# Rotary projection as 128 stationary columns: weight halves side by side, summed by VectorE

## The reference, cut to what matters

```python
x = layernorm(x)                      # (8, 512, 512)
c_kv = x @ W_DKV + b_DKV              # 512 -> 128
c_q  = x @ W_DQ  + b_DQ               # 512 -> 128
k_c, v_c, q_c = c_kv @ W_UK + b_UK, c_kv @ W_UV + b_UV, c_q @ W_UQ + b_UQ
k_r = (x @ W_KR + b_KR) * pe          # 512 -> 32, the rotary part, shared by 16 heads
q_r = (x @ W_QR + b_QR) * pe          # 512 -> 32
k = concat([k_c per head, k_r]);  q = concat([q_c per head, q_r])
attn = softmax(q @ k.T / sqrt(32));  ctx = attn @ v_c;  y = ctx @ W_O + b_O
```

## Time and profile before

| | us |
|---|---|
| median of 3 runs | 1569.3 (1569.14 to 1573.41) |
| profiled execution, its span | 1566.3 |
| PE busy | 1498.5 (96%) |
| DVE busy | 974.3 (62%) |
| POOL busy | 803.9 (51%) |
| ACT busy | 783.3 (50%) |

### The profile page before, as it was taken

One profiled execution on the slowest core, in us unless ns is written; L12 is line 12 of the kernel. 1 busy time (PEld: TensorE's weight loads), 2 busy tenths in 40 slices (PEclk: granted clock), 3 DMA queues, 4 the chain that ended last, 5 costly groups with the idle time before them and its releaser, 6 DMA issues.

```text
span 1566.3 us, 21725 instructions
## 1 busy us (share of the span) xinstructions
PE 1498.5 (96%) x7006; PEld 1018.5 (65%) x7006; DVE 974.3 (62%) x1841; ACT 783.3 (50%) x1415; POOL 803.9 (51%) x812
## 2 busy tenths in 40 slices
PE   5699999999999999999998999999999999999998
PEld 3355666656656666566564578778666666668886
DVE  3657676767676767767667454862333333349988
ACT  3265567566565675665647455422222222275554
POOL 1076787787776977877859630003222222143341
PEclk9699999999999999999999999999999999999999
DMA  5878669589495795884956421536987777697773
GB/s 130 138 100 135 101 109 213 74 173 172 82 179 111 121 211 74 181 156 85 222 97 129 135 79 67 198 121 196 311 235 219 210 215 221 195 349 241 232 241 125
DMA packets 163926, 257.75 MB, mean 165 GB/s; under 512 B 20100, under 2 KB 70404, under 8 KB 161764
## 3 DMA queue, kind: packets, MB, share of 16 engines
q1 hardware_dynamic: 144584, 204.98, 58.0%
q0 software_dynamic: 12784, 41.82, 9.4%
q10 hardware_dynamic: 6448, 9.57, 1.8%
HBM read 103.74 MB, written 58.46 MB: 104 GB/s over the span
## 4 chain that ended last, share of the span: by engine, by line
PE 71%; DMA 10%; DVE 7%; POOL 4%; issue 3%; ACT 2%; SPq 2%; DVEq 0%; POOLq 0%; ACTq 0%
PE bank L113 12%; PE bank L724 9%; PE bank L792 8%; PE bank L815 8%; PE bank L646 6%; PE bank L632 6%; DMA a<-a 6%; PE bank L662 6%; PE bank L651 6%; PE bank L746 5%; POOL a L1637 2%; PE bank L671 2%; DMA f<-f 1%; SPq L1875 1%; PE bank L804 1%
## 5 line engine op out<-in xcount | busy, mean ns | idle before, releaser
L1637 POOL TENSOR_TENSOR a<-a 128x512 f32<-128x512 f32 x384 | 499.5, 1329 | 100.2 <-ACT a L1443 54.5
L1443 ACT ACTIVATE a<-bank 128x512 f32<-128x512 f32 x512 | 296.4, 597 | 258.4 <-PE bank L651 218.4
L925 DVE TENSOR_REDUCE a<-bank 128x1 f32<-128x512 f32 x512 | 321.3, 680 | 80.2 <-PE bank L632 79.7
L113 PE MATMUL bank<-a 128*128 128x512 f32 (+1 forms) x864 | 238.9, 398 | 2.7 <-DVE s L877 1.6
L646 PE MATMUL bank<-a 128*128 128x512 f32 x512 | 217.3, 424 | 5.0 <-ACT a L1443 4.9
L651 PE MATMUL bank<-a 68*128 68x512 f32 x512 | 203.8, 398 | 0.4 <-ACT a L1433 0.2
L632 PE MATMUL bank<-a 128*128 128x512 f32 x512 | 181.0, 425 | 22.7 <-DMA a<-a 17.8
L113 PEld LDWEIGHTS bank<-a 128*128 128x128 f32 (+1 forms) x864 | 158.9, 186 | 49.1 <-issue 6.7
L1701 POOL DMA_INDIRECT f<-h_scratch,f x79 | 75.4, 954 | 224.5 <-DMA f<-f 203.6
L746 PE MATMUL bank<-c 128*128 128x512 f32 x768 | 178.2, 391 | 4.2 <-DVE c L983 2.1
L724 PE MATMUL bank<-c 128*128 128x512 f32 x768 | 177.4, 390 | 1.3 <-ACT c L1484 1.3
(11 more groups left out here) (190 smaller groups left out, 1766.9 us busy)
## 6 DMA issues: line engine op xcount, KB each, us to landing
a<-a SPq DMA_DIRECT2D x272, 256.0 KB, 9.7
f<-f SPq DMA_DIRECT2D x316, 64.0 KB, 3.9
yp_scratch<-f SPq DMA_DIRECT2D x79, 256.0 KB, 3.4
a<-in_L_attn_x SPq DMA_DIRECT2D x15, 1024.0 KB, 11.7
x_scratch<-a SPq DMA_DIRECT2D x8, 1024.0 KB, 4.6
h_scratch<-a SPq DMA_DIRECT2D x8, 1024.0 KB, 13.3
hT_scratch<-s SPq DMA_DIRECT2D x8, 1024.0 KB, 9.8
c<-hT_scratch SPq DMA_DIRECT2D x8, 1024.0 KB, 7.0
```

Source lines behind the costliest of these rows:

```text
L113: t = e.matmul(out, a[n], b[n], start=n == 0 and m == 0, stop=n == len(ah) - 1 and m == 2)
L925: e.tensor_reduce(K.mx[:, i, j:j + 1], K.MX[n % 3][:], AX.X, ALU.max).then_inc(Z.max, 1)
L1443: e.activation(K.pt[:, n % NP, :], K.SC[n % 2][:], ACT.Exp, scale=SCALE).then_inc(Z.exp, 1)
L1637: e.tensor_tensor(K.acc[:, j, :], a, K.pt[:, n % NP, :], ALU.add).then_inc(Z.acc, 1)
```

## The change

The rotary weights leave `K.wd` and get a tile of their own, `K.wdr` [128, 4, 64]. `K.wdh` grows from 320 to 384 columns and holds their high part and, beside it, their low part; `K.wdl` loses them. On PE, 4 matmuls with both parts as 128 stationary columns against the high tokens write all 128 partitions of the bank, and 4 with the 64 high columns against the low tokens add to the first 64. ACT gets a new instruction for every batch: it takes the bank's last 64 partitions (low weights x high tokens), adds the bias and writes `K.krq`; it takes over the waits for `Z.cx` and `Z.rope`. DVE then adds the first 64 partitions of the bank to `K.krq` and multiplies by `K.pe` as a second instruction; the rounding and the subtraction stay. At the start ACT rounds and DVE subtracts in two instructions each instead of one.

```diff
@@ attention_room, shared_room
-    K.wdl = tile([P, 4, WD], F32R)
-    K.wdh = tile([P, 4, WD], F32R)
+    K.wdl = tile([P, 4, WL], F32R)
+    K.wdh = tile([P, 4, WH], F32R)
...
+    K.wdr = tile([P, 4, 2 * HD])
@@ tensor_program, proj
+        w.wait_ge(Z.w_r, 1)
...
+        if what == "r":
+            blocks = lambda a: a.rearrange("p (i s) -> p i s", s=P)
+            low = tokens(K.xnl)
+            both = [K.wdh[:, k, at:at + 2 * n] for k in range(4)]
+            e.matmul(blocks(bank[:]), both[0], high[0], start=True, stop=False)
+            for k in range(4):
+                e.matmul(blocks(bank[0:n, :]), K.wdh[:, k, at:at + n], low[k], start=False, stop=False)
+            for k in range(1, 4):
+                t = e.matmul(blocks(bank[:]), both[k], high[k], start=False, stop=k == 3)
+            t.then_inc(*end("proj", b, "r"))
+            return
@@ vector_program, split_w and proj
+        if what == "d":
+            e.tensor_tensor(K.wdh[:, :, WL + 2 * HD:], K.wdr, K.wdh[:, :, WL:WL + 2 * HD], ALU.subtract).then_inc(Z.w_r, 1)
...
-        if b:
-            w.wait_ge(Z.rope, 3 * b)
-            w.wait_ge(Z.cx, NG * (b - 1) + 2)
-        e.scalar_tensor_tensor(out=K.krq, in0=bank[0:2 * HD, :], scalar=K.br[:], in1=K.pe[:],
-                               op0=ALU.add, op1=ALU.mult).then_inc(*end("proj", b, "r"))
+        w.wait_ge(Z.r_low, b + 1)
+        e.tensor_tensor(K.krq, bank[0:2 * HD, :], K.krq, ALU.add).then_inc(*end("proj", b, "r"))
         n = K.fill["proj", b, "r"]
         w.wait_ge(Z.free[n % 2], n // 2 + 1)
+        e.tensor_tensor(K.krq, K.krq, K.pe[:], ALU.mult).then_inc(Z.r_sum, 1)
+        w.wait_ge(Z.r_sum, b + 1)
@@ scalar_program, split_w and proj
             w.wait_ge(Z.w1, 4 * 16)
+            e.copy(K.wdh[:, :, WL:WL + 2 * HD], K.wdr).then_inc(Z.w_hi, 1)
...
+        bank = begin("proj", b, what)
         if what == "r":
+            w.wait_ge(Z.w1b, 6 * 16)
+            if b:
+                w.wait_ge(Z.rope, 3 * b)
+                w.wait_ge(Z.cx, NG * (b - 1) + 2)
+            e.activation(K.krq, bank[2 * HD:4 * HD, :], ACT.Identity, bias=K.br[:]).then_inc(Z.r_low, 1)
             return
```

More of the change, by code:

```diff
@@ L40 @@
 VS = 5
-WD = 2 * LAT + 2 * HD
+WL = 2 * LAT
+WH = 2 * LAT + 4 * HD
 COLS = {"kv": (0, LAT), "q": (LAT, LAT), "r": (2 * LAT, 2 * HD)}
@@ L371, in __init__ @@
         self.KR, self.stack = many("KR_in", 2), many("stack_in", RS)
-        self.QR, self.w_hi, self.w_lo = many("QR_in", 2), make("w_high"), make("w_low")
+        self.QR, self.w_hi, self.w_lo, self.w_r = many("QR_in", 2), make("w_high"), make("w_low"), make("w_rotary_low")
         self.xn_hi, self.c_hi, self.cx_hi, self.cx_lo = make("xn_high"), make("c_high"), make("ctx_high"), make("ctx_low")
@@ L380, in __init__ @@
         self.dT = make("dT_done")
+        self.r_low, self.r_sum = make("rotary_low_part"), make("rotary_sum")
         self.scaled = {k: make(f"scaled_{k}") for k in KINDS}
@@ L457, in shared_room @@
     K.xnl = tile([P, 4, D], F32R)
-    K.wd = tile([P, 4, WD])
-    tile([P, 4 * WD + 4 * S])
+    K.wd = tile([P, 4, WL])
+    tile([P, 4 * WH + 4 * S])
     K.wu = tile([P, 3, D])
@@ L868, in split_w @@
     def split_w(what):
-        given, high, low, n = {"d": (K.wd, K.wdh, K.wdl, 1), "u": (K.wu, K.wuh, K.wul, 2), "o": (K.wo, K.woh, K.wol, 3)}[what]
+        given, high, low, n = {"d": (K.wd, K.wdh[:, :, 0:WL], K.wdl, 2), "u": (K.wu, K.wuh, K.wul, 3), "o": (K.wo, K.woh, K.wol, 4)}[what]
         w.wait_ge(Z.w_hi, n)
+        if what == "d":
+            e.tensor_tensor(K.wdh[:, :, WL + 2 * HD:], K.wdr, K.wdh[:, :, WL:WL + 2 * HD], ALU.subtract).then_inc(Z.w_r, 1)
         e.tensor_tensor(low, given, high, ALU.subtract).then_inc(Z.w_lo, 1)
@@ L1369, in split_w @@
     def split_w(what):
-        given, high = {"d": (K.wd, K.wdh), "u": (K.wu, K.wuh), "o": (K.wo, K.woh)}[what]
+        given, high = {"d": (K.wd, K.wdh[:, :, 0:WL]), "u": (K.wu, K.wuh), "o": (K.wo, K.woh)}[what]
         if what == "d":
             w.wait_ge(Z.w1, 4 * 16)
+            e.copy(K.wdh[:, :, WL:WL + 2 * HD], K.wdr).then_inc(Z.w_hi, 1)
         elif what == "u":
@@ L1397, in proj @@
     def proj(b, what):
+        bank = begin("proj", b, what)
         if what == "r":
+            w.wait_ge(Z.w1b, 6 * 16)
[3 more added lines that the diff above has]
+            e.activation(K.krq, bank[2 * HD:4 * HD, :], ACT.Identity, bias=K.br[:]).then_inc(Z.r_low, 1)
             return
-        bank = begin("proj", b, what)
         n, bias_ = (0, K.bdkv) if what == "kv" else (1, K.bdq)
@@ L1748, in sync_program @@
     e.dma_start(K.ident[:], ins["c_ident"]).then_inc(Z.ident, 16)
-    for name, (at, n) in (("L0_attn_W_DKV", COLS["kv"]), ("L0_attn_W_DQ", COLS["q"]), ("L0_attn_W_KR", (2 * LAT, HD)),
-                          ("L0_attn_W_QR", (2 * LAT + HD, HD))):
-        e.dma_start(K.wd[:, :, at:at + n], w4(name)).then_inc(Z.w1, 16)
+    for name, room, at, n in (("L0_attn_W_DKV", K.wd, 0, LAT), ("L0_attn_W_DQ", K.wd, LAT, LAT), ("L0_attn_W_KR", K.wdr, 0, HD),
+                              ("L0_attn_W_QR", K.wdr, HD, HD)):
+        e.dma_start(room[:, :, at:at + n], w4(name)).then_inc(Z.w1, 16)
     for n, name in enumerate(("L0_attn_W_UK", "L0_attn_W_UQ", "L0_attn_W_UV")):
```

## The result

| | before | after |
|---|---|---|
| median, us (runs) | 1569.3 (5) | 1598.24 (5; 1597.69 to 1600.97) |
| profiled execution, its span, us | 1566.3 | 1596.4 |
| mean granted TensorE clock | 0.988 | 0.975 |

The ratio is 1.0183, with a 95% interval of 1.0168 to 1.0198: the change makes the kernel 28.7 us slower (26.4 to 31.1). The forecast was 1598.4 us.

A forecast was written before the change was run, and what follows sets the result against it. PE was taken to set the pace in the attention. Longer chain less transfer waits +19.0, clock +9.9, start-up +0.2: +29.1 us on the 1566.3 us span gives 1595.4, and 3.0 more for the median 1598.4 us; range 1575 to 1606.

The forecast's parts named there:

- What bounds the kernel: In the attention PE sets the pace; its waits are small, under 10 us together, and any longer wait is paid in full.
- PE's part is worth nothing: Four rotary matmuls fewer save PE 0.92 us a batch, which only turns into waiting: worth 0 in batches 1 to 7.
- The chain: DVE's rotary chain ends at T + 5.51 (T: end of POOL's divide), 3.19 us longer, with two turns lost to POOL.
- The transfer waits are absorbed: PE's six transfer waits about 15 us behind the rotary steps, 3.3 us together, absorb their own length of the delay.
- Rival A: In DVE's rotary chain no turn is lost to POOL: 1.24 us longer, 1575.2 us, up to 1585 with the clock; chance 0.17.
- The clock: Behind each of seven PE stops at least one half-clock stretch follows, 1.4 us each (bounds 0.5 to 2.5): +9.9 us.
- The start-up: At the start, ACT's rounding in two instructions costs one more fixed part: +0.2 us, on the path.
- The sum: For the whole kernel, 19.0 + 9.9 + 0.2 = +29.1 us on the profiled span of 1566.3 us, giving 1595.4.
- B: Behind PE's stops the clock doesn't fall; the forecast's chain alone gives 1588.5 us; chance 0.10.
- C: The last two copies land 3.2 us later, so the 3.3 us of transfer waits aren't absorbed: 1601.7 us; chance 0.04.
- D: Row maxima that PE doesn't need yet take up DVE's delay: -1.8 us, 1567.5 us, no change; chance 0.06.
- E: PE, the busiest engine, loses 32 matmuls from its total: 7.4 us less, 1562.1 us; chance 0.08.

The follow-up runs named there:

- DVE held: The kernel before, with two or five unread bn_stats on DVE behind the rotary subtraction in batches 1 to 7: ratio 1.0076 with two, 1.0162 with five.
- the kernel with short additions: The kernel after, with POOL's two additions beside the rotary chain cut to one of 512 columns: ratio 1.0049.
- The kernel with the rounding on ACT: The kernel after, with row maxima between the steps of DVE's rotary chain and the rounding done by ACT instead of DVE: ratio 0.9995.
- PE's part alone: The kernel before, with the change's 8 rotary matmuls and 128 stationary columns, DVE's old three instructions and no new ACT instruction: ratio 1.0029.
- before with row maxima between: The kernel before, with two row maxima ahead of the rounding and two ahead of the subtraction in DVE's old rotary chain: ratio 1.0072.

## Why the prediction was right, point by point

- **What bounds the kernel.** Right. PE's small waits were paid in full when they grew. The kernel with DVE held shows it alone.
- **PE's part is worth nothing.** Right as a sum, but "nothing" was the lucky side. By itself it costs: the earlier scores close the 0.41 us gap ahead of POOL's addition, and the old subtraction loses the turn that it had won by 0.02 us. The prediction used that 0.02 us row for the old chain and didn't ask what an earlier PE does to it.
- **The chain.** Right by each step. It was to end at T + 5.51, 3.19 us later; it ends at T + 5.52, and PE's bank comes 3.21 us later. Product and rounding took 1.70 and 1.37 us, where 1.6 and 1.4 were worked out. The two runs that take POOL or one DVE instruction away show that the turns are the cause. The Trainium skill, "SBUF — State Buffer", section "SBUF: two separate sides", calls the shared pair an exclusive lock that the first to start keeps. By that rule the trace agrees: the product that starts 0.12 us behind POOL ends 0.55 us behind POOL's end, and takes 684 ns when POOL is out of the way.
- **The transfer waits are absorbed.** Right. None of the six is left, and the one of 0.78 us at 426.76 us is gone too, so the term was 4.1 us and not 3.3. (Rival A took 3.0 us for the same waits.) That the copies come later by 3.2 us costs nothing that the rows show.
- **The clock.** The mechanism was right, the term mis-sized in the profiled run. One stretch was priced for each stop, 1.4 us. Six periods had 11 stretches at about 1.1 us, and they left 2.05 us for each stop, inside the bounds of 0.5 to 2.5.
- **The start-up.** The +0.2 us isn't there. ACT's timeline of after:

```profile
11.09 0.40 ACT L1389 CAST a<-s 128x256 fp32r<-128x256 f32 x1 [9.07 <-DMA s<-in_L_attn_W_QR]
11.40 1.04 ACT L1395 CAST a<-s 128x1024 fp32r<-128x1024 f32 x1
```

  The second starts 0.09 us before the first ends, and both together end at 12.44, as the one instruction of before does. The fixed part of 0.19 us, worked out from longer and shorter instructions, overlaps at least in part with the instruction ahead.
- **The sum.** It was +29.1 us on the span, and +30.1 is measured; seven periods by 4.60 would be 32.2, and the first step comes 2.27 us earlier in after (T 125.35 against 127.62). I don't count that as a gain of the change: T of the first step lies anywhere between those two and 127.82 in the other profiled runs, at 125.94 and at 127.82 for the two kernels with DVE held, which have the old start-up and the old rotary step. So the closeness of 1598.4 to 1598.24 is in part luck: over the six periods the clock term was too small by 3.9 us, the transfer waits gone were too small by 0.8 us, and the start came out early. The timed runs say 28.7 us (26.4 to 31.1), of which 7 x 3.20 less 4.1, 18.3 us, is settled by the rows. The other 10.4 us hold the clock, batch 0 and what follows the attention, and the timed runs don't divide them further.
- **The rivals.** A is out for after, and the kernel with short additions shows what it would have been: stop 2.39 us (2.4 worked out), low clock in some batches. B is out by PEclk, C and D by the missing transfer waits and the stop. E is the one whose first step is true, 32 matmuls less, but PE waits for what lies behind POOL's divide. The kernel with the rounding on ACT shows that even a chain that PE hardly waits for doesn't bring it about; in batches 1, 3, 5 and 6 the transfers end the next wait.

## What to carry to other kernels

Before taking work off the busiest engine, look at what its next wait is released by: a saving ahead of a released wait turns into waiting, and it can move another engine's work into the turn of a third. Where DVE's SBUF work and POOL's share one stretch, cost a chain by the turns that POOL has ready, not by the sum of the instructions' own times. A stop of PE costs more than its length when half clock follows it, so a long DVE chain in front of row maxima is better cut into pieces, and its rounding put on ACT, if every piece is checked against POOL's turns.

## What the runs showed of the hardware that was not expected

- **Half clock behind short stops.** Stops of PE of 1.45, 1.57 and 1.75 us were followed by 3.4 us at PEclk 0.50 in three of six batches each, stops of 2.05 us in four of six, of 2.39 us in five of six. Of the stops of 3.36 us and more, each was followed by one or two such stretches. Near 165 us three kernels (PE's part alone, POOL short, before with row maxima between) have one more such stretch, behind two waits for ACT of about 0.64 and 0.35 us; before and after have the same two waits and stay at full clock. Equal stops in equal surroundings differed, so the length of the stop isn't all that decides; what does was not settled.
- **A rounding copy takes turns too.** DVE's fp32 to fp32r copy, with one SBUF input, takes 0.42 us alone and 0.65 to 1.53 us beside POOL's additions. It ends 0.28 us behind the end of POOL's addition in before and after, the two-input instructions 0.55 us.
- **A near miss can turn over.** An order won by 0.02 us held in all seven batches of before, a saving of 0.92 us on PE turned it over in all seven, and with DVE held by two instructions it turned over by itself in the last of seven.
